# Copying the second half of the next pair's merged queries behind the eighth unit's exponentials instead of ahead of the seventh's

## The reference, cut to what matters

```
q_nope = (q_latent @ q_b_w.T).reshape(B, S, N_HEADS, D_NOPE)
q_rope = (q_latent @ q_rope_w.T).reshape(B, S, N_HEADS, D_ROPE)
...
q = jnp.concatenate([q_nope, q_rope], axis=-1)
...
scores = jnp.einsum('bqhd,bkhd->bhqk', q, k) * scale
probs = jax.nn.softmax(scores, axis=-1)
attn = jnp.einsum('bhqk,bkhd->bqhd', probs, v)
```

## Time and profile before

| what | value |
|---|---|
| median of 3 runs | 699.37 us (697.64 to 700.8) |
| the profiled execution | 699.7 us |
| its span, first to last instruction | 697.5 us |
| PE busy | 672.3 us, 96% |
| DVE busy | 489.4 us, 70% |
| ACT busy | 424.1 us, 61% |
| mean granted clock of PE | 0.995 of full |

### The profile page before, as it was taken

How to read it: one execution, slowest core, us unless ns; L and a number is a source line. 1 busy time by engine, 2 the same in 40 slices (tenths; PEclk the granted TensorE clock), 3 DMA queues, 4 the chain that set the end, 5 groups by cost and what they waited for, 6 DMA issues and landing times.

```text
span 697.5 us, 13846 instructions
## 1 busy us (share of the span) xinstructions
PE 672.3 (96%) x4756; PEld 584.0 (84%) x4756; DVE 489.4 (70%) x1418; ACT 424.1 (61%) x1099; POOL 297.5 (43%) x301
## 2 busy tenths in 40 slices
PE   5999999999999999999999989999989999999997
PEld 3778888888889898887888856566889999999997
DVE  6897877777867787777797877777465555644544
ACT  3856168788797878888654778888654213222221
POOL 0584154646465555542165228997343410400000
PEclk9999999999999999999999999999999999999999
DMA  8903044453535444351920000200300000000000
GB/s 325 351 0 99 4 133 120 162 173 106 170 117 163 129 152 126 103 157 60 357 90 0 1 2 14 95 1 3 121 1 1 1 3 16 1 16 1 1 16 16
DMA packets 26725, 59.43 MB, mean 85 GB/s; under 512 B 3146, under 2 KB 12748, under 8 KB 26272
## 3 DMA queue, kind: packets, MB, share of 16 engines
q1 hardware_dynamic: 23584, 50.35, 21.2%
q0 software_dynamic: 3072, 8.20, 3.5%
HBM read 48.24 MB, written 10.49 MB: 84 GB/s over the span
## 4 chain that ended last, share of the span: by engine, by line
PE 77%; DVE 13%; ACT 5%; issue 4%; DMA 0%; POOL 0%; SPq 0%; DVEq 0%; ACTq 0%
PE bank L2255 11%; PE bank L2020 7%; PE bank L1954 6%; PE bank L2278 6%; PE bank L2011 5%; PE bank L2304 5%; PE bank L2040 3%; PE bank L1961 3%; PE bank L2116 3%; PE bank L2031 3%; PE bank L2082 3%; PE bank L2224 3%; PE bank L2318 2%; PE bank L2208 2%; PE bank L2163 2%
## 5 line engine op out<-in xcount | busy, mean ns | idle before, releaser
L1063 ACT ACTIVATE sb<-bank,sb 128x256 f32<-128x256 f32 x128 | 59.6, 471 | 40.7 <-DVE sb L1559 38.8
L1559 DVE TENSOR_REDUCE sb<-bank 128x2 f32<-128x512 f32 x64 | 43.7, 683 | 47.5 <-PE bank L2020 47.1
L1265 ACT ACTIVATE h_parts<-sb 128x256 fp32r<-128x256 f32 x56 | 23.4, 418 | 71.3 <-DVE sb L1809 43.4
L2020 PE MATMUL bank<-sb 128*128 128x256 f32 x256 | 66.1, 381 | 0.0
L1800 DVE TENSOR_TENSOR sb<-sb,bank 128x256 f32<-128x256 f32 x56 | 23.5, 419 | 58.9 <-ACT sb L1228 58.9
L2255 PE MATMUL bank<-rounded,b_hi 128*128 128x256 f32 x224 | 63.5, 283 | 0.0
L2255 PE MATMUL bank<-am_lo,b_hi 128*128 128x256 f32 x224 | 63.3, 283 | 0.0
L2255 PE MATMUL bank<-rounded,b_lo 128*128 128x256 f32 x224 | 63.3, 283 | 0.0
L1228 ACT ACTIVATE sb<-bank 128x256 f32<-128x256 f32 x56 | 21.5, 383 | 63.4 <-PE bank L2255 63.3
L835 POOL DMA_INDIRECT expert_out<-sb x32 | 33.0, 1032 | 60.3 <-DVE sb L1501 46.9
L1070 ACT ACTIVATE sb<-sb 128x256 f32<-128x256 f32 x128 | 57.7, 503 | 0.1
(11 more groups left out here) (321 smaller groups left out, 1974.2 us busy)
## 6 DMA issues: line engine op xcount, KB each, us to landing
sb<-in_w_gate_up SPq DMA_DIRECT2D x32, 368.0 KB, 3.0
sb<-in_w_down SPq DMA_DIRECT2D x32, 256.0 KB, 2.7
sb<-in_w_pair SPq DMA_DIRECT2D x8, 704.0 KB, 4.1
expert_out<-sb SPq DMA_DIRECT2D x1, 4096.0 KB, 22.2
sb<-expert_out SPq DMA_DIRECT2D x8, 512.0 KB, 7.4
sb<-in_w SPq DMA_DIRECT2D x1, 1792.0 KB, 13.7
sb<-in_b SPq DMA_DIRECT2D x1, 1792.0 KB, 8.0
sb<-in_sw_up SPq DMA_DIRECT2D x1, 1536.0 KB, 9.1
```

Source lines behind the costliest of these rows:

```text
L1063: act.activation(probs[:, u % 4, q, :], bank[3 + u % 2][:, q * S:(q + 1) * S], ACT.Exp, scale=-1.0, bias=row_min[:, u % 4, q:q + 1], accum ...
L1559: dve.tensor_reduce(row_min[:, u % 4, :], bank[3 + u % 2][:, :].rearrange("p (q n) -> p q n", q=QT), AX.X, ALU.min).then_inc(at_min, 1)
L2020: mm = pe.matmul(bank[3 + u % 2][:, q * S:(q + 1) * S], qb[i][:, h, b * S + q * P:b * S + (q + 1) * P], keys[:, h, b * S:(b + 1) * S], sta ...
```

## The change

ACT copies the second half of the next pair's merged queries one unit later, and behind instead of ahead of that unit's exponentials. The first half stays in unit 4, and no other engine's order changes.

```diff
                 experts(p, u, 0)
-                if p + 1 < PAIRS and u in (4, 6):
-                    merged_queries(p + 1, (u - 4) // 2, (p + 1) % 2, bank[0])
+                if p + 1 < PAIRS and u == 4:
+                    merged_queries(p + 1, 0, (p + 1) % 2, bank[0])
                 act.wait_ge(at_min, g + 1)
                 at_least(act, at_t, g - 3)
                 for q in range(QT):
                     act.activation(probs[:, u % 4, q, :], bank[3 + u % 2][:, q * S:(q + 1) * S], ACT.Exp, scale=-1.0,
                                    bias=row_min[:, u % 4, q:q + 1], accum_out=row_sum[:, u % 4, q:q + 1])\
                         .then_inc(at_exp, 1)
+                if p + 1 < PAIRS and u == 7:
+                    merged_queries(p + 1, 1, (p + 1) % 2, bank[0])
```

## The result

The changed kernel is slower by a seventh of a per cent: 699.6 us median of 22 runs (697.96 to 700.9) against 698.28 us for the kernel before, timed beside it in 22 runs (697.53 to 700.8). The ratio is 1.0014, with a 95% interval of 1.0007 to 1.0020, which is +1.0 us (+0.5 to +1.4). The forecast was no change that can be told at 0.5%, with +1.6 us as its sum and 701.0 us as its time.

The account below looks back on a forecast made before the run. PE was taken to bound the kernel, busy 30.82 of 31.00 us a pair. Terms -0 + 1.0 + 0.6 = +1.6 us, giving 701.3 on the profiled execution and 701.0 against the median; range 698.3 to 703.4 us.

Parts of the forecast that it names:

- Nothing won in unit 6: Unit 6, ACT: the copies lie under the exponentials' wait for the row minimum, so removing them gains 0.
- 1.18 us added in unit 7: Unit 7, ACT: two copies of 0.59 us each, without overlap, delay the normalising of unit 6 by 1.18 us.
- The tanh and the hidden layer late by 1.18 and 0.49: Next pair's unit 0: ACT's tanh moves 1.18 us later, and DVE's hidden layer behind it starts 0.49 us late.
- the prediction's lower bound: With a copy pair of 1.08 us: hidden layer 0.39 late, gate product 0.07, last boundary 0.49; loss 0.9 us.
- 0.17 us a boundary through the copy of the turned rows: Unit 1: DVE's late copy of the turned rows makes PE's gate product lose 0.17 us at six boundaries, 1.0 us.
- 0.6 us in series at the seventh boundary: Pair 6, unit 7: copies make the tanh 0.59 us late, all in series through DVE to PE's gate product.
- Who does not wait: PE's merging product, which needs bank 0, does not wait for the copies: they end 1.7 us ahead of it.
- The rival of a slower kernel: DVE's 0.49 us delay is carried, not regained in unit 2: 3.5 us lost, 702.9 us; chance 0.08.
- The sum: Whole kernel: 0 gained, 1.0 us lost at six boundaries, 0.6 at the seventh; +1.6 us, making 701.0 us.
- the forecast case: Whole kernel: a loss between the bounds of 0.9 and 2.5 us; chance 0.60.
- The absorbed rival: Copies overlap, six boundaries lose 0.03 us or less, the seventh 0.45: 0.6 us in all, 700.0 us; chance 0.27.

Follow-up runs that it names:

- hidden_first: Kernel before, but in unit 6 DVE forms the expert's hidden layer ahead of the row minimum instead of behind it; timed ratio 0.9966.
- tanh_ahead: Changed kernel, but in unit 0 ACT takes the tanh ahead of low context and high part; trace distance 303.18 us against 302.60 before, not timed.
- pair_6: Kernel before with the copies moved in pair 6 only (the seventh boundary); timed ratio 1.0006, trace +0.71 us.
- next_unit_0: Second-half copies put in unit 0 of the next pair, behind its tanh and ahead of its exponentials, against the kernel before; timed ratio 1.0059.
- double_7: Changed kernel with the two copies done twice in unit 7; timed ratio 1.0134 against the kernel before.
- hidden_first_7: Changed kernel (copies in unit 7 behind the exponentials), with DVE's hidden layer ahead of the minimum in unit 6; 702.74 us against 698.19 for before.
- behind_normal: Changed kernel with the unit 7 copies moved behind the normalising of unit 6 as well; trace +1.59 us against the kernel before, not timed.
- pairs_0_5: Kernel before with the copies moved in pairs 0 to 5 only, pair 6 left as it was; timed ratio 1.0002, trace +0.51 us.

## Why the prediction was right, step by step

- **Nothing won in unit 6.** Shown by the trace: exponentials 0.72 to 0.73 us behind the minimum's start with the copies and without, ACT idle for 1.21 us. One reading was too short: the chain that ended last holds more than three DVE lines. From 203.00 to 207.13 us it runs through DVE alone, the hidden layer (L1506, L1508, L1509) among them, and that stretch is what hidden_first shortens.
- **1.18 us added in unit 7.** Measured 1.22: 0.60 from copy to copy and 0.62 from the second copy to the normalising, the follower for which there was no row. It does not overlap with the copy, so the estimated 1.04 us that the page "ScalarE: Activation LUTs" of the Trainium skill (section What ACT_TABLE_LOAD costs) would make of the pair by its overlap of about 93 ns is not what happens here.
- **The tanh and the hidden layer late by 1.18 and 0.49.** Measured 1.07 and 0.37. This is the term that was mis-sized. The normalising is 1.21 us late, the low context only 1.09: it starts 0.81 us behind the normalising's start in the changed kernel (208.81 to 209.62) and 0.93 before (207.37 to 208.30), so that 0.12 us of the delay is caught up there. The hidden layer then stands where the prediction's lower bound has it (0.39), but that bound got there by a shorter pair of copies, which the trace does not show: that its loss of 0.9 us is nearly the one measured is luck.
- **0.17 us a boundary through the copy of the turned rows.** The place and the releaser are as predicted (a wait on PE's weight load that was not there, L1497), the size is 0.07: six boundaries 0.4 us instead of 1.0. Of the 0.17, 0.07 was a later start, which did not come, and 0.10 a longer group, of which 0.08 to 0.09 came. tanh_ahead shows that this loss hangs on the tanh alone.
- **0.6 us in series at the seventh boundary.** Measured 0.6, and 0.6 at the place itself in pair_6.
- **Who does not wait.** PE's merging product did not wait for the copies. next_unit_0 shows that it does once they end later.
- **The rival of a slower kernel** priced the delay as carried from pair to pair. It is not: the periods are all alike. But double_7 and hidden_first_7 show its price where the cover of 0.3 us is gone: over 1 us a pair.
- **The sum.** The trace's +1.0 us lies inside the forecast case (0.9 to 2.5), near its lower end; the +1.6 us of the sum lies just above the timed interval of +0.5 to +1.4, and the median of 699.6 just below the likeliest 700 to 702, for the term above and the lower median of the kernel before. The absorbed rival (+0.6) is not what happened: the six boundaries lost 0.07 us each, not 0.03 or less.

## What to carry to other kernels

An engine that is 61% busy can still have stretches without a gap; what an instruction costs there is decided by the first thing behind it that another engine waits for, not by the queue's idle time elsewhere. Put work that nobody is in a hurry for into the wait for an operand (here ahead of the exponentials, under the row minimum), where it is free, and look at the cover behind the place before moving it. The same 1.2 us a pair cost 1.0 us in all in the change, 4.5 in next_unit_0, 6.6 in hidden_first_7, and, put on top of the change in double_7, another 8.7, depending on what cover was left. And compare traces at a mark inside the span: here two executions with equal spans differed by 1.0 us in the part that was changed.

## What the runs showed of the hardware that had not been expected

Two scaled copies of 64 x 512 out of the same bank, one into partitions 0 to 63 and one into 64 to 127, started 0.60 us apart and the next instruction 0.62 us behind the second, with a length of 0.59: no overlap. The 0.62 does not depend on what follows: it is there for the normalising (208.19 to 208.81), for a tanh (302.48 to 303.10), for the exponentials in next_unit_0 (211.71 to 212.33) and for the low context in behind_normal (304.21 to 304.83). Two ACT copies of 128 x 256 (L1072) took 0.91 us together with a length of 0.50 each. Whether the change of partitions or another trait keeps the copies from overlapping was not tried. The low context follows the normalising at 0.81 to 0.82 us wherever the copies stand directly ahead of the normalising and the low context directly behind it (six boundaries each in the change, pairs_0_5, double_7 and hidden_first_7), and at 0.91 or more everywhere else in the pair loop; in tanh_ahead, where the tanh takes the low context's place behind the same copies and normalising, it follows at 0.93 (207.82 to 208.75). The cause stays open.
